# Two attention stages with heads of 8: raw projections copied out of PSUM first, keys and outputs turned in pairs, VectorE order changed

## What is computed

```python
# L1 (stage s=2, kind 1): one shared key and value head, causal
latent = x @ Wc_down
q = (latent @ Wq_up).reshape(B, T, 16, 8)
k, v = split(latent @ Wkv_up)                 # 8 channels each, shared by all heads
att = softmax(where(causal, einsum('bthd,bsd->bhts', q, k) / sqrt(8), -inf))
y = einsum('bhts,bsd->bthd', att, v).reshape(B, T, 128) @ Wc_proj

# L3 (stage s=6, kind 3): own keys and values, causal with a window of 128 tokens, biases
q, k, v = split(x @ w_in.T + b_in)            # 16 heads of 8 each
scores = where((j <= i) & (j >= i - 128), q @ k.T / sqrt(8), -1e9)
y = (softmax(scores) @ v).reshape(B, T, 128) @ w_out.T + b_out
```

## Time and profile before

| | us |
|---|---|
| median of 3 runs | 2583.11 (2582.85 to 2583.80) |
| profiled execution, its own time | 2596.31 |
| its span, first to last instruction | 2594.7 |
| mean granted clock of TensorE, share of full speed | 0.972 |
| stage s=2, from its first statistics to its last `XR` addition | about 886 to 1188 |
| stage s=6, likewise | about 2216 to 2547 |

### The profile page before, as it was taken

One profiled execution on the slowest core, in us unless ns is written; L12 is line 12 of the kernel. 1 busy time (PEld: TensorE's weight loads), 2 busy tenths in 40 slices (PEclk: granted clock), 3 DMA queues, 4 the chain that ended last, 5 costly groups with the idle time before them and its releaser, 6 DMA issues. The chain is left out here.

```text
span 2594.7 us, 62276 instructions
## 1 busy us (share of the span) xinstructions
PE 2388.0 (92%) x23977; PEld 1854.6 (71%) x23977; DVE 1684.9 (65%) x4424; ACT 1477.3 (57%) x3068; POOL 1575.1 (61%) x2498
## 2 busy tenths in 40 slices
PE   5999999999999789988999999999999968788897
PEld 5888888888886456656777787778777757455555
DVE  6677677777784377774545467777777622577676
ACT  4666666666664367764444466666666523466665
POOL 5787787777785344443433267777777721666664
PEclk9999999999999879999999999999999979899999
DMA  8940000000000000000000000000000045000000
GB/s 268 328 144 2 2 2 2 2 2 2 2 2 1 21 25 2 2 2 20 13 1 1 3 4 4 6 6 4 6 6 6 5 137 173 15 10 8 8 4 33
DMA packets 23111, 83.10 MB, mean 32 GB/s; under 512 B 4097, under 2 KB 11010, under 8 KB 21794
## 3 DMA queue, kind: packets, MB, share of 16 engines
q1 hardware_dynamic: 19666, 71.90, 8.6%
q0 software_dynamic: 3152, 7.21, 0.9%
HBM read 71.89 MB, written 46.79 MB: 46 GB/s over the span
## 5 line engine op out<-in xcount | busy, mean ns | idle before, releaser
L906 POOL TENSOR_TENSOR XR<-XR,T 128x256 f32<-128x256 f32 x512 | 376.3, 735 | 151.3 <-DVE T L785 121.1
L656 ACT ACTIVATE P<-ps 128x384 f32<-128x384 f32 (+1 forms) x512 | 250.6, 542 | 179.0 <-PE ps L2598 176.2
L2598 PE MATMUL ps<-P,V 128*64 128x256 f32 (+3 forms) x4096 | 333.5, 347 | 10.4 <-DVE O L1392 8.4
L1376 DVE TENSOR_REDUCE bm<-ps 128x3 f32<-128x384 f32 x512 | 260.2, 550 | 114.9 <-PE ps L2598 114.2
L2598 PEld LDWEIGHTS ps<-P,V 128*64 128x64 f32 (+1 forms) x4096 | 185.7, 123 | 132.0 <-issue 35.3
L1311 ACT ACTIVATE P<-ps 128x768 f32<-128x768 f32 x256 | 207.7, 811 | 99.4 <-PE ps L2598 98.5
L796 DVE TENSOR_REDUCE sm<-ps 128x2 f32<-128x512 f32 (+1 forms) x256 | 130.8, 553 | 174.5 <-PE ps L2598 173.9
L1476 POOL TENSOR_SCALAR_AFFINE_SELECT P<-P 128x512 f32<-128x512 f32 x256 | 162.3, 634 | 123.2 <-ACT P L1311 120.6
L919 POOL TENSOR_TENSOR PS<-P 128x256 f32<-128x256 f32 x256 | 181.6, 735 | 70.8 <-ACT P L656 70.5
L2598 PE MATMUL ps<-mk,identb 128*128 128x256 bf16 (+1 forms) x1024 | 205.2, 294 | 13.0 <-DVE bm L1376 10.8
L927 POOL TENSOR_TENSOR ss<-ss,nhalf 128x16 f32<-128x16 f32 x64 | 187.7, 2933 | 5.3
(11 more groups left out here) (309 smaller groups left out, 7017.4 us busy)
## 6 DMA issues: line engine op xcount, KB each, us to landing
rows_i<-in_zero SPq DMA_DIRECT2D x16, 1208.0 KB, 31.2
rows_o<-in_zero SPq DMA_DIRECT2D x16, 1208.0 KB, 80.5
w<-in_m_w SPq DMA_DIRECT2D x23, 578.0 KB, 4.0
zt<-rows_i SPq DMA_DIRECT2D x23, 128.0 KB, 3.2
rows_o<-yo POOLq DMA_DIRECT2D x23, 128.0 KB, 3.8
stg<-in_t_w SPq DMA_DIRECT2D x11, 256.0 KB, 2.8
XR<-in_x SPq DMA_DIRECT2D x4, 512.0 KB, 8.9
out<-XR SPq DMA_DIRECT2D x8, 256.0 KB, 2.0
```

The lines of the kernel that those rows point to most:

```text
L656: e.activation(self.P[at % 6][:, :], K.ps.ap("st", s, g, h)[:, 0:self.w], ACT.Exp, bias=0.0, scale=1.0 if kind == 0 else 0.125).then_inc(K ...
L906: p = po.e.tensor_tensor(x, x, self.T[g % 2][:, par, pr], ALU.add)
L1376: e.tensor_reduce(bm[:, h, :], K.ps.ap("mx", s, g, h)[:, 0:384].rearrange("p (a c) -> p a c", c=128), X, ALU.max, negate=True).then_inc(K. ...
L2598: return self.te.matmul(o, l, r, start=start, stop=True, skip_group_check=True)
```

## The change

It is confined to `Narrow` and acts in both kinds.

- Raw: one ScalarE copy takes the whole `raw` bank to a new SBUF tile `rf` and gives the bank back. One tick later ScalarE writes hi from `rf` (two instructions in place of four), VectorE's lo reads `rf` and hi (two in place of four) and GpSimd's copies follow. A new semaphore `lo_in` stands for lo done; the turns wait for it, and the next copy into `rf` waits for the lo of the block before. In kind 1 the values come from `rf` too.
- Keys of kind 3: the four transposes of two units go into one bank, and one ScalarE copy of 512 columns takes them out, once per two units.
- Outputs: `pT` of two units (four transposes, one bank) at the step k=18 of the second, then one reciprocal of 16 columns and one multiplication of 128; `Ts` gets a fourth buffer.
- VectorE's order within a tick: `O` first, then the maxima, then the rest, and the steps k < 3 of a block (statistics, normalization) last.

```diff
-        self.dve_order = ticks(items, lambda name, k: not (name == "unit" and k in (3, 4)))
+        self.dve_order = ticks(items, self.dve_rank)
+    def dve_rank(self, name, k):
+        if name == "unit":
+            return 0 if k == 18 else 1 if k in (3, 4) else 2
+        return 3 if name == "prep" and k < 3 else 2
...
     def pe_turned(self, pe, ps, b, parts):
-        pe.wait_ge(*K.ps.read("raw", self.s, b))
+        pe.wait_ge(self.lo_in, b + 1)
         pe.wait_ge(self.qk8, b + 1)
...
         if k == 0:
-            if kind == 3:
-                self.pe_turn(pe, b, self.ka[b % 3][:, :, 4 * u:4 * u + 4, :], "kz", s, g)
+            if kind == 3 and u % 2 == 0:
+                ps = K.ps.take(pe, self.G, *self.kz_name(b, u))
+                for n in range(2):
+                    p = self.pe_turned(pe, ps[:, 256 * n:256 * n + 256], b,
+                                       self.ka[b % 3][:, :, 4 * (u + n):4 * (u + n) + 4, :])
+                p.then_inc(K.ps.full_of(*self.kz_name(b, u)), 1)
...
-        if k == 18:
-            ps = K.ps.take(pe, self.G, "pT", s, g)
-            pe.wait_ge(*K.ps.read("pv", s, g))
-            for i in range(2):
-                p = K.tr(ps[:, 128 * i:128 * i + 128], self.Ts[g % 3][:, 128 * i:128 * i + 128])
-            p.then_inc(K.ps.full_of("pT", s, g), 1)
+        if k == 18 and u % 2:
+            ps = K.ps.take(pe, self.G, "pT", s, g // 2)
+            for n in range(2):
+                pe.wait_ge(*K.ps.read("pv", s, g - 1 + n))
+                for i in range(2):
+                    o = 256 * i + 128 * n
+                    p = K.tr(ps[:, o:o + 128], self.Ts[(g - 1 + n) % 4][:, 128 * i:128 * i + 128])
+            p.then_inc(K.ps.full_of("pT", s, g // 2), 1)
...
         if k == tk["raw"]:
+            if b >= 1:
+                ac.wait_ge(self.lo_in, b)
+            ac.wait_ge(*K.ps.filled("raw", s, b))
+            e.activation(self.rf[:, :, :].rearrange("p t c -> p (t c)"),
+                         K.ps.ap("raw", s, b)[:, 0:288 if kind == 1 else 512], ACT.Copy).then_inc(
+                K.ps.out_of("raw", s, b), 1)
+        if k == tk["raw"] + 1:
...
-            for t in range(2):
-                e.activation(self.qa[b % 3][:, t, :, 0:8], rq[:, t], ACT.Copy)
-            for t in range(2):
-                i = e.activation(self.ka[b % 3][:, t, :, 0:8], rk[:, t], ACT.Copy)
-            i.then_inc(self.hi_in, 1)
+            e.activation(self.qa[b % 3][:, :, :, 0:8], rq, ACT.Copy)
+            e.activation(self.ka[b % 3][:, :, :, 0:8], rk, ACT.Copy).then_inc(self.hi_in, 1)
...
-        if k == tk["raw"]:
+        if k == tk["raw"] + 1:
             dv.wait_ge(self.hi_in, b + 1)
-            for t in range(2):
-                e.tensor_tensor(ka[:, t, :, 16:24], rk[:, t], fv(ka[:, t, :, 0:8]), ALU.subtract)
-            for t in range(2):
-                i = e.tensor_tensor(qa[:, t, :, 8:16], rq[:, t], fv(qa[:, t, :, 0:8]), ALU.subtract)
-            i.then_inc(K.ps.out_of("raw", s, b), 1)
+            e.tensor_tensor(ka[:, :, :, 16:24], rk, fv(ka[:, :, :, 0:8]), ALU.subtract)
+            e.tensor_tensor(qa[:, :, :, 8:16], rq, fv(qa[:, :, :, 0:8]), ALU.subtract).then_inc(self.lo_in, 1)
...
-                if k == self.tk["raw"]:
+                if k == self.tk["raw"] + 1:
                     qa, ka = self.qa[b % 3], self.ka[b % 3]
                     po.wait_ge(*self.cleared(b))
                     po.wait_ge(self.hi_in, b + 1)
```

More of the change, by code:

```diff
@@ L1000, in __init__ @@
         self.ka = [sb(f"ka{s}_{i}", [128, 2, 4 if kind == 1 else 16, 32], F32R) for i in range(3)]
-        self.kz = [sb(f"kz{s}_{i}", [128, 256], F32R) for i in range(4 if kind == 1 else 8)]
+        self.kz = [sb(f"kz{s}_{i}", [128, 256 if kind == 1 else 512], F32R) for i in range(4)]
+        self.rf = sb(f"rf{s}", [128, 2, 144 if kind == 1 else 256], F32)
         self.qq = [sb(f"qq{s}_{i}", [128, 512], F32R) for i in range(4)]
@@ L1004, in __init__ @@
         self.P = [sb(f"P{s}_{i}", [128, 2, 512], F32) for i in range(6)]
-        self.Ts = [sb(f"Ts{s}_{i}", [128, 256], F32) for i in range(3)]
+        self.Ts = [sb(f"Ts{s}_{i}", [128, 256], F32) for i in range(4)]
         self.O = [sb(f"O{s}_{i}", [128, 2, 128], F32) for i in range(3)]
         self.OT = [sb(f"OT{s}_{i}", [128, 256], F32) for i in range(2)]
-        self.rs = [sb(f"rs{s}_{i}", [128, 8], F32) for i in range(2)]
+        self.rs = [sb(f"rs{s}_{i}", [128, 16], F32) for i in range(2)]
         self.V = [sb(f"V{s}_{i}", [128, 2, 32 if kind == 1 else 168], F32) for i in range(4)]
         self.clear, self.hi_in, self.qk8 = (K.sem(f"{n}{s}") for n in ("clear", "hi_in", "qk8"))
+        self.lo_in = K.sem(f"lo_in{s}")
         self.v_in, self.masked, self.least = K.sem(f"v_in{s}"), K.sem(f"masked{s}"), K.sem(f"least{s}")
@@ L1032, in y, with kz_name @@
         return "y", self.s, b
+    def kz_name(self, b, u):
+        return "kz", self.s, b if self.kind == 1 else 2 * b + u // 2
     def kz_of(self, b, u):
-        return b if self.kind == 1 else 4 * b + u
+        if self.kind == 1:
+            return self.kz[b % 4]
+        return self.kz[(2 * b + u // 2) % 4][:, 256 * (u % 2):256 * (u % 2) + 256]
     def pe(self, pe):
@@ L1178, in pe_scores @@
         if mx is not None:
-            pe.wait_ge(*K.ps.read("kz", s, at))
+            pe.wait_ge(*K.ps.read(*self.kz_name(b, u)))
             pe.wait_ge(*K.ps.read(*self.qq_name(g)))
@@ L1200, in pe_final @@
             ps = K.ps.take(pe, self.G, "OT", s, b)
-            for u in range(4):
-                pe.wait_ge(*K.ps.read("pT", s, 4 * b + u))
+            for n in range(2):
+                pe.wait_ge(*K.ps.read("pT", s, 2 * b + n))
             for i in range(2):
@@ L1290, in act_unit @@
         if k == 0:
-            if self.kind == 3:
+            if self.kind == 3 and u % 2 == 0:
                 if g >= 8:
-                    ac.wait_ge(*K.ps.filled("st", s, g - 8, 1))
-                self.act_turn(ac, self.kz[g % 8], "kz", s, g)
+                    ac.wait_ge(*K.ps.filled("st", s, g - 7, 1))
+                ac.wait_ge(*K.ps.filled(*self.kz_name(b, u)))
+                e.activation(self.kz[g // 2 % 4][:, :], K.ps.ap(*self.kz_name(b, u))[:, :], ACT.Copy).then_inc(
+                    K.ps.out_of(*self.kz_name(b, u)), 1)
             if g < 3:
@@ L1383, in dve_unit @@
                 e.tensor_tensor(nm, m[:, 0:2], m[:, 0:3:2], ALU.min).then_inc(self.least, 1)
[L1384 to L1387, removed]
+        if k == 18 and u % 2:
+            v = K.ps.ap("pT", s, g // 2)[:, :].rearrange("p (a c) -> p a c", c=32)
+            rs = self.rs[g // 2 % 2]
+            dv.wait_ge(*K.ps.filled("pT", s, g // 2))
             n = dv.step(e.reciprocal(rs[:, :], v[:, :, 8]))
             dv.after(n)
-            if b >= 3 and u == 0:
+            if b >= 3 and u == 1:
                 dv.wait_ge(*K.ps.filled("OT", s, b - 3))
[L1392 to L1395, removed]
+            o = 64 * (u // 2)
+            e.tensor_tensor(self.O[b % 3][:, :, o:o + 64].rearrange("p t (a c) -> p t a c", c=8),
+                            v[:, :, 0:8].rearrange("p (t a) c -> p t a c", t=2),
+                            rs[:, :].rearrange("p (t a) -> p t a", t=2).unsqueeze(3).to_broadcast([128, 2, 8, 8]),
+                            ALU.mult).then_inc(K.ps.out_of("pT", s, g // 2), 1)
     def dve_final(self, dv, b, k):
```

27 lines of the change are left out of this document (10 added, 17 removed).

## The result

The changed kernel takes 2561.88 us (median of 4, 2558.24 to 2564.22) against 2583.45 for the kernel before (median of 4): ratio 0.9913, 95% interval 0.9896 to 0.9930, or 21.6 us less. The sum of the prediction was 23. The profiled execution takes 2563.29 us (span 2561.7, mean granted clock 0.971), 1.4 above its median where that of before was 13 above; so the two profiles differ by 33 us, and 21.6 is what the runs show. The profiled execution of before (2596.31 us) is slower than every other execution of that kernel on record (2578 to 2589 us), so differences between the two profiles come out too large.

What follows compares the result with a forecast made beforehand. TensorE, busy 93% (kind 1) and 88% (kind 3), was taken as the bound. Gains of 6.5 us in kind 1 and 18.5 in kind 3, minus 2 for starts, make 23: 2583 to 2560 us, range 2527 to 2578.

Steps and rivals of the forecast that it cites:

- the new wait at the query turn: Kind 3, TensorE's `qq` two ticks after `raw`: new waiting for lo and GpSimd's casts, 1.2 us a block, ends 0 and 2.4.
- the lower bound: Kind 3's query turn: casts end at 4.9 us, TensorE arrives at 4.1, so at least 0.8 us of waiting.
- the upper bound: Kind 3's query turn: lo, held behind GpSimd's masks and casts like the normalization, ends at 5.7 us; wait 1.6.
- I let the 0.50 for the exponential go: Kind 3: TensorE's 0.50 us a block wait for the exponential vanishes, because it follows the stall for `O`; ends 0 and 0.5.
- `O` first: VectorE's `O` before the maxima, with a shorter ring: TensorE's waits for `O` go, 0.65 us a block (kind 1), 0.87 (kind 3).
- Raw's bank now needs one copy ... Wait gone: 1.37 per block: Kind 3: ScalarE's copy frees the bank at 1.0 us, next taker near 1.9, so the 1.37 wait for lo goes.
- I cost all this at nothing: Changed VectorE and ScalarE instruction counts priced at zero, neither being the bound; VectorE has about 0.8 us a block less.
- The sentence on scores that come closer together: Ticks without `pT` bunch scores, which then wait for the exponential or a maximum; in exchange `O` delays maxima less.
- In kind 1 I let nothing go: Kind 1: no change counted in waits from bunched scores, where a score tick already waits 0.6 us for maxima.
- The hold: Lo held by GpSimd's masks and casts; rivals: held every block, 2574 us, chance 0.17; slower still, 2600 us, 0.07.
- The overlapped block: Kind 1's block overlapping the next stage's statistics, 21.2 us at clock 0.78: counted 0, up to 5 us to gain.
- The starts: Start of each stage: an extra copy and hi a tick later lose about 1 us each, between 0.5 and 2.

Runs made afterwards that it cites:

- experiment 3: The change with outputs turned one unit at a time again, as before the change: 2547.7 us, ratio 0.9861.
- experiment 4: The change with kind 3's keys turned one unit at a time again, as before the change: 2555.8 us, ratio 0.9890.
- experiment 5: The change without the raw copy (hi and lo read PSUM at raw's tick), its two-input minimum of the maxima made a one-input reduction: 2532.2 us, ratio 0.9798.
- experiment 2: The change with VectorE's old order (maxima first in every tick, then the rest in list order): 2570.2 us, ratio 0.9944.
- experiment 10: The kernel before plus O first, hi and lo as one instruction each and the one-input minimum; no raw copy, no pairs: 2548.2 us, ratio 0.9868.
- experiment 11: The kernel before plus O first, joined hi and lo, one-input minimum and kind 3's keys in pairs; no raw copy, no output pairs: 2537.0 us, ratio 0.9817.
- experiment 6: The whole change, with the minimum of the maxima as a one-input reduction: 2552.5 us, ratio 0.9878.
- experiment 1: The change without the raw copy: hi and lo read the PSUM bank at raw's tick, two-input minimum kept: 2569.9 us, ratio 0.9941.
- experiment 8: The change with hi, lo and GpSimd's casts moved back to the tick of raw, raw copy kept: 2595.6 us, ratio 1.0044.

## Why the prediction was right, and where it was not

**The total** is right: 21.6 us measured, 23 forecast, and the case forecast (15 to 40 us) is the one that came. Against its own profiled time, the profile of after lies 10 us below the 2573 of the sum. That 21.6 and 23 lie so close is partly luck: between the profiles the two stages gained 29.4, and terms that were wrong offset each other, as follows.

**Kind 3**, 18.1 us forecast and 17.98 measured: the waits for lo and `O` went, and the new wait at the query turn is 1.1 where 1.2 was taken. Its chain is as forecast: GpSimd's casts come after both masks, and they, not lo, end last, as in the lower bound. That bound, 0.8, had the masks undisturbed; beside lo they take about 0.4 longer. Lo is not held by whole masks, as the upper bound had it, but by 0.2 us once (in experiments 3 and 4 by 0.43 at the second lo). The example behind that bound, the normalization, reads one tensor and a statistic (`z<-XR,stat`), not two tensors as lo and the minimum do, so it was a weak example of the pair that the Trainium skill's rule in the prediction is about.

One term failed: "I let the 0.50 for the exponential go". It did not go but rose to 0.65 (7.2 us in eleven blocks). Without the copy it is 0.78 (8.6 us, experiment 5), so the copy does not explain it. With the unforeseen 0.4 for the minimum, about 1.0 us a block was lost that the sum did not have. Waits that it did not list made up 0.7 of this. They are, in before (2290.85 to 2506.5) and then after (2271.48 to 2469.30):

```profile
PEld ps L2598 <- DVE bm L1376: 5.0, 10, 0.6
PEld ps L2601 <- ACT OT L1286: 4.5, 11, 0.4
PEld ps L2598 <- ACT qq L1304: 2.1, 9, 0.2
```

```profile
PEld ps L2615 <- DVE bm L1392: 2.2, 11, 0.3
PEld ps L2618 <- ACT OT L1305: 2.1, 11, 0.2
```

So 17.98 beside 18.1 is luck in part.

**Kind 1**, 15.5 forecast and 14.93 measured. The new wait is 0.48, not 0.65; a wait of weight loads for the copy to `zT`, 0.42 us a block before, which I had not listed, is gone; and the wait for maxima fell from 0.65 to 0.57. That is 0.17 + 0.42 + 0.08 = 0.67 against the 0.57 between forecast and result.

**`O` first** is worth 0.67 in kind 1 (experiment 2; 0.65 forecast) and 0.46 in kind 3 (0.87). The step mis-sized is the second: with pairs the next taker is already two ticks away, so only the maxima behind a late `O` are left to gain.

**The step that failed** is "Raw's bank now needs one copy ... Wait gone: 1.37 per block". The wait went, but the copy was not needed for it. Experiment 5 has no copy and no such wait, because pairs alone put the next taker of the bank far enough back (experiments 10, 11 and 5 in turn). The raw copy then costs 20 us (experiments 5 and 6). I counted one wait, two remedies, and one price, without asking which remedy carried it.

**"I cost all this at nothing"**, of turns in pairs: beside the copy the output pairs cost 0.38 and 0.69 us a block and the key pairs 0.54 in kind 3, part of it through the held minimum; with the one-input minimum both together cost 0.41 and 0.29. The sentence on scores that come closer together named the mechanism, and then "In kind 1 I let nothing go" put it at zero. These costs were hidden in the total by gains that were not forecast.

**The hold.** The prediction looked for VectorE held by GpSimd at lo. It was there, by 0.2 us in kind 3 and 0.47 in kind 1 (the addition of `y` keeps its 0.41), but in kind 3 it cost most at the smallest instruction, whose median gave no sign: 0.175 us, with 2.63 the longest, and that only in kernels 1 and 8. In the change it takes 0.87 at most. What one would say from experiment 1 alone, that the raw copy gains 8 us, is true of this kernel, and only because hi, lo and casts stand a tick later there. The copy itself does not help: experiment 8 has it without the later tick, and its longest minimum is 2.63 again.

**The overlapped block** gained 4.0 of the up to 5 that were left open, in one execution of each kernel. The starts lost 2 as forecast, but not 1 each: kind 1 gained 1.0 and kind 3 lost 3.1.

What stays open: why the clock falls in the last blocks of kind 3 after the change; no run tried that, nor the starts. Open too is how the 20 us of the raw copy divide between its delay and lo's new place in SBUF.

## What to carry to other kernels

Where two parts of a change cure the same wait, run each without the other: the second may bring only its price. When undoing a part makes a kernel slower, look at which instruction got longer before crediting the part; here a held minimum of 128x8 elements hid that the raw copy costs 20 us. And a short operation that stands between two engines is worth building with one operand in SBUF, if GpSimd works on SBUF beside it: that edit alone gave 9 us before and after the change, and 38 without the raw copy. (It changed the instruction too, a reduction for a two-input minimum; no run separates the two.)

## What the runs showed of the hardware

Beside masks the two-input minimum takes up to 2.63 us (experiments 1 and 8), the reduction 0.171 to 0.174 in all 44 cases (experiment 5). The Trainium skill ("SBUF — State Buffer", Who interferes with whom) says that a VectorE instruction with two SBUF inputs and a GpSimd instruction that reads SBUF exclude each other, and that a reduction never contends on trn2; in that much the trace agrees. Two things differ from a wait for one instruction to finish. The minimum stood through five masks in a row (2.27 us; the longest mask is 0.64). And lo and a mask that started within 10 ns of each other both grew: the two lo from 0.42 + 0.42 to 0.42 + 0.63, the masks from 0.42 + 0.64 to 0.67 + 0.81. In kind 1 a lo of 128x64 elements took 0.686 us beside a mask, against 0.21 in experiment 8, where it stood elsewhere.
